# A state-space layer with a routed feed-forward block: chunk 0's second delta, gate projections and a later chunk's statistics go into the prologue, its taps into the steady order, and the gate's silu to step 8

## The reference, cut to what matters

```python
x = x + ssm(layernorm(x))      # x: 8 sequences x 1024 tokens x 256 features, fp32
x = x + ffn(layernorm(x))

def ssm(x):
    xp, z = split(x @ in_proj.T)                   # 512 channels each
    xc = silu(causal_conv(xp, conv_w))             # 4 taps per channel, along time
    dt, B, C = split(xc @ x_proj.T)                # 64, 16, 16 columns
    delta = softplus(dt @ dt_proj.T + dt_b)
    hs[t] = exp(delta * A) * hs[t-1] + delta * B * xc     # 512 channels x 16 states
    y = sum over the states (hs * C) + D * xc
    return (y * silu(z)) @ out_proj.T
```

## Time and profile before

| | before |
|---|---|
| median of 3 runs | 1596.67 us (1594.35 to 1600.29) |
| the profiled execution: time, span of its instructions | 1596.78 us, 1594.7 us |
| busy: DVE, PE, POOL, ACT | 93%, 91%, 88%, 79% |
| first scan starts (end of the prologue) | 40.73 us |
| first scan of chunk 1 starts | 148.48 us |

### The profile page before, as it was taken

One profiled execution on the slowest core, in us unless ns is written; L12 is line 12 of the kernel. 1 busy time (PEld: TensorE's weight loads), 2 busy tenths in 40 slices (PEclk: granted clock), 3 DMA queues, 4 the chain that ended last, 5 costly groups with the idle time before them and its releaser, 6 DMA issues.

```text
span 1594.7 us, 39330 instructions
## 1 busy us (share of the span) xinstructions
PE 1454.2 (91%) x15138; PEld 1124.9 (71%) x15138; DVE 1476.0 (93%) x1773; ACT 1257.9 (79%) x2100; POOL 1409.8 (88%) x1248
## 2 busy tenths in 40 slices
PE   7788999999999999999999999999999999998876
PEld 4466767677776777767777777777777777776765
DVE  4789999999999999999999999999999999998884
ACT  6778697897978879797887979789796987877651
POOL 2679899999989999899999989899998999999993
PEclk9999999999999999999999999999999999999998
DMA  4203013040320404022040311304031030403201
GB/s 136 80 2 112 23 29 134 3 160 2 95 68 3 159 3 147 15 69 94 3 159 3 130 32 43 120 3 160 2 101 61 16 133 3 147 1 93 69 15 41
DMA packets 78511, 106.46 MB, mean 67 GB/s; under 512 B 42289, under 2 KB 67761, under 8 KB 70130
## 3 DMA queue, kind: packets, MB, share of 16 engines
q1 hardware_dynamic: 78322, 103.92, 20.3%
HBM read 86.10 MB, written 17.30 MB: 65 GB/s over the span
## 4 chain that ended last, share of the span: by engine, by line
ACT 27%; DVE 25%; PE 23%; issue 15%; POOL 9%; SPq 1%; DVEq 0%; DMA 0%; ACTq 0%; POOLq 0%
DVE hs L919 22%; ACT da L586 12%; PE BX L233 9%; POOL hs L1203 6%; PE Y L257 3%; PE Y L282 3%; PE PB L357 2%; PE PB L330 2%; ACT xc L653 1%; ACT gate L647 1%; ACT u L691 1%; ACT L663 1%; ACT L662 1%; ACT u L689 1%; ACT u L693 1%
## 5 line engine op out<-in xcount | busy, mean ns | idle before, releaser
L1203 POOL TENSOR_TENSOR hs<-hs,cb 128x1024 f32<-128x1024 f32 x512 | 1209.8, 2364 | 70.3 <-DVE hs L919 49.6
L919 DVE TENSOR_TENSOR_SCAN hs<-da,BX 128x512 f32<-128x512 f32 x1024 | 1165.6, 1201 | 70.1 <-PE BX L233 61.4
L586 ACT ACTIVATE da<-delta,a_neg 128x511 f32<-128x511 f32 (+1 forms) x1024 | 665.3, 712 | 34.4 <-DVE hs L919 34.0
L257 PEld LDWEIGHTS Y<-ident,hs 128*128 128x128 f32 x4096 | 470.7, 142 | 95.7 <-issue 61.7
L257 PE MATMUL Y<-ident,hs 128*128 128x128 f32 x4096 | 518.5, 275 | 9.5 <-POOL hs L1203 9.3
L233 PE MATMUL BX<-bd,uT 32*128 32x128 f32 x8192 | 302.3, 284 | 91.0 <-DVE hs L919 86.9
L233 PEld LDWEIGHTS BX<-bd,uT 32*128 32x128 f32 x8192 | 253.2, 187 | 149.6 <-DVE hs L919 142.0
L282 PE MATMUL Y<-xnT,w_in 128*128 128x512 f32 x240 | 119.2, 620 | 2.1 <-ACT gate L639 2.0
L307 PE MATMUL PA<-w_in,xnT 128*128 128x512 f32 x240 | 115.6, 604 | 0.0
L621 ACT ACTIVATE xp<-Y 128x512 f32<-128x512 f32 x60 | 35.9, 598 | 93.5 <-PE Y L282 93.0
L1199 POOL COPY hlast<-hs 128x2 f32<-128x2 f32 x256 | 47.9, 187 | 55.8 <-DVE hs L919 54.0
(11 more groups left out here) (177 smaller groups left out, 1511.4 us busy)
## 6 DMA issues: line engine op xcount, KB each, us to landing
cb<-c_scratch SPq DMA_DIRECT2D x64, 1024.0 KB, 4.8
x<-in_x SPq DMA_DIRECT2D x16, 512.0 KB, 3.9
x_scratch<-x2T SPq DMA_DIRECT2D x16, 512.0 KB, 6.6
xt<-in_x SPq DMA_DIRECT2D x15, 512.0 KB, 4.0
bd<-bt SPq DMA_DIRECT2D x480, 1.0 KB
out<-x SPq DMA_DIRECT2D x15, 512.0 KB, 3.3
...
c_scratch<-dbc SPq DMA_DIRECT2D x64, 8.0 KB, 1.5
```

The lines of the kernel that those rows point to most:

```text
L257: mm = e.matmul(Y[(G * c + g) % 2][:, t * P:(t + 1) * P], hs[:, k % HR, q, t * P:(t + 1) * P], ident[:, :], is_transpose=True, start=False ...
L586: e.activation(da[:, k % DR, q, h:], delta[:, g, h:], ACT.Exp, scale=a_neg[:, g, n:n + 1]).then_inc(s_da, 1)
L919: e.tensor_tensor_scan(hs[:, k % HR, q, :], da[:, k % DR, q, :], BX[:, :].rearrange("p (t n) -> p n t", n=RT)[:, n % RT, :], float(c % HV) ...
L1203: e.tensor_tensor(hs[:, k % HR, :, :], hs[:, k % HR, :, :], cb[:, Q * p:Q * p + Q, :], ALU.mult).then_inc(s_hc, 1)
```

## The change

In the prologue, DVE's two memsets come first and no longer wait for the weights; ACT waits only for `w_conv` before the convolution, and its exponential of `A_log` stands behind the copy of `dbc`; PE runs 24 instead of 16 matmuls on the identity, transposes chunk 0 block by block as the norm hands it over, and runs three more on the identity. Delta of group 1 (into a bank of BX), its `pool_u`, the last two gate projections, the transposes of chunk 1 (now behind the first BX) and the statistics of chunk 3 are in the prologue or placed anew there. In chunk 0 the four projections stand at steps 0, 4, 8, 12 instead of 0, 2, 6, 12, and the taps are split: two at 1, 5, 9, 13 and the third at 3, 7, 9, 15. In every chunk the gate's silu moves from step 1 to step 8, the transposes of chunk c+2 from steps 3 and 5 to 2 and 3, `act_norm` from step 27 to 31, `pool_rstd` from 23 to 25.

```diff
-BANK_B = {0: [("o", -2, 0)], 2: [("ut", 0, 1)], 3: [("trc", 2, 0)], 4: [("yt", -1, 2)], 5: [("trc", 2, 1)], 6: [("dt", 0, 2)],
-          8: [("res", -1, 0)], 15: [("yt", 0, 0)], 16: [("dt", 0, 3)], 20: [("ut", 0, 3)], 21: [("yt", 0, 1)], 24: [("dt", 1, 0)],
+BANK_B = {0: [("o", -2, 0)], 2: [("ut", 0, 1), ("trc", 2, 0)], 3: [("trc", 2, 1)], 4: [("yt", -1, 2)], 6: [("dt", 0, 2)],
+          8: [("res", -1, 0)], 13: [("trc0", 2, 1)], 15: [("yt", 0, 0)], 16: [("dt", 0, 3)], 20: [("ut", 0, 3)], 21: [("yt", 0, 1)], 24: [("dt", 1, 0)],
...
+            if (stage, c, i) == ("dt", 0, 1):
+                return BX[:, CH:2 * CH], 0, s_d1, s_d1_out
...
+        def pe_trc_first(e):
+            for t in range(TB):
+                if t < TB - 1:
+                    e.wait_ge(s_xn0, t + 1)
+                else:
+                    e.wait_ge(s_xn, 1)
+                for kk in range(KD):
+                    mm = e.transpose((PB, PA)[kk][:, t * P:(t + 1) * P], xt[:, t, kk * P:(kk + 1) * P], ident[:, :])
+                    if t == TB - 1:
+                        mm.then_inc((s_pb, s_pa)[kk], 1)
...
-            for _ in range(16):
+            for _ in range(24):
...
-            pe_trc(e, 0, 0)
-            pe_trc(e, 0, 1)
+            pe_trc_first(e)
+            for _ in range(3):
+                e.matmul(Y[1][:, 0:P], ident[:, :], ident[:, :], start=True, stop=True)
...
-                    if c == 0 and s in (0, 2, 6, 12):
-                        pe_xp(e, (4, 5, 6, 7)[(0, 2, 6, 12).index(s)])
+                    if c == 0 and s in (0, 4, 8, 12):
+                        pe_xp(e, G + s // 4)
...
-                    if s == 3 and c and on(c + 2):
+                    if s == 2 and c and on(c + 2):
                         pe_trc(e, c + 2, 0)
...
-                    if s == 5 and c and on(c + 2):
+                    if s == 3 and c and on(c + 2):
                         pe_trc(e, c + 2, 1)
...
             act_norm(e, 1)
-            e.wait_ge(s_wt, 16 * 10)
...
+            e.wait_ge(s_wc, 16)
+            act_halo(e, 0)
+            act_xp_first(e, 0)
+            act_xp_first(e, 1)
+            e.preload_act_table(ACT.Silu)
+            act_silu_first(e, 0)
+            act_xp_first(e, 2)
+            act_xp_first(e, 3)
...
+            e.preload_act_table_set(EXPS)
+            act_dbc(e, 0)
...
                     if s == 1 and c:
                         act_z(e, c, 3)
-                        act_silu_z(e, c)
...
-                    if s == 1 and c == 0:
-                        act_silu_z(e, 0)
+                    if s == 8:
+                        act_silu_z(e, c)
...
-                    if s == 27 and on(c + 3):
+                    if s == 31 and on(c + 3):
                         act_norm(e, c + 3)
...
-                    if c == 0 and s == 1:
-                        dve_delta(e, 0, 1)
-                    if c == 0 and s in (1, 5, 9, 15):
-                        for kk in range(K - 1):
-                            dve_tap(e, (4, 5, 6, 7)[(1, 5, 9, 15).index(s)], kk)
+                    if c == 0:
+                        if s in (1, 5, 9, 13):
+                            dve_tap(e, G + s // 4, 0)
+                            dve_tap(e, G + s // 4, 1)
+                        if s in (3, 7, 9, 15):
+                            dve_tap(e, {3: G, 7: G + 1, 9: G + 2, 15: G + 3}[s], 2)
```

More of the change, by code:

```diff
@@ L69, in mamba_moe @@
     x2_dram = nc.dram_tensor("x2_scratch", (NQ, P, KD, CH), F32, kind="Internal").ap()
-    a_use = bank_uses(BANK_A, NQ, S, [("trc", 0, 1), ("trc", 1, 1), ("dbc", 0, 0), ("bt", 0, 0), ("dt", 0, 1)])
-    b_use = bank_uses(BANK_B, NQ, S, [("trc", 0, 0), ("trc", 1, 0), ("dt", 0, 0), ("ut", 0, 0)])
+    a_use = bank_uses(BANK_A, NQ, S, [("trc", 0, 1), ("dbc", 0, 0), ("bt", 0, 0), ("trc", 1, 1)])
+    b_use = bank_uses(BANK_B, NQ, S, [("trc", 0, 0), ("dt", 0, 0), ("ut", 0, 0), ("trc", 1, 0)])
     def on(c):
@@ L293, in pe_xp_first, with pe_z_first @@
             mm.then_inc(s_x0, 1)
-        def pe_z_first(e, t):
+        def pe_z_first(e, t, parts=range(2)):
             if t >= 2:
                 e.wait_ge(s_z0_out, t - 1)
-            for kk in range(KD):
+            for kk in parts:
                 mm = e.matmul(Y[t % 2][:, :], xnT[0][:, kk, t * P:(t + 1) * P], w_in[:, kk, ED:2 * ED], start=(kk == 0),
                               stop=(kk == KD - 1))
-            mm.then_inc(s_z0, 1)
+            if kk == KD - 1:
+                mm.then_inc(s_z0, 1)
         def pe_z(e, c, t):
@@ L328, in pe_dt @@
             e.wait_ge(out, n)
+            if (c, g) == (0, 1):
+                e.wait_ge(s_xc0, 2)
             e.wait_ge(s_pa_out, a_use["dbc", c, 0] + 1)
@@ L432, in tensor @@
             pe_dbc(e, 0, 1)
+            pe_z_first(e, 3, (0,))
             pe_dt(e, 0, 0)
             pe_bt(e, 0)
+            pe_dt(e, 0, 1)
+            pe_z_first(e, 3, (1,))
             pe_z_first(e, 2)
             pe_ut(e, 0, 0)
+            e.wait_ge(s_d1_out, 1)
             pe_bx(e, 0)
-            pe_dt(e, 0, 1)
-            pe_z_first(e, 3)
+            pe_trc(e, 1, 0)
+            pe_trc(e, 1, 1)
             for c in range(NQ):
@@ L755, in scalar @@
             e.wait_ge(s_ident, 1)
-            act_norm(e, 0)
+            e.wait_ge(s_sh, 1)
+            for t in range(TB):
+                e.activation(xt[:, t, :], xt[:, t, :], ACT.Identity, bias=shift[:, t:t + 1],
+                             scale=rstd[:, t:t + 1]).then_inc(s_xn0 if t < TB - 1 else s_xn, 1)
             act_trc(e, 0, 0)
@@ L795, in scalar @@
                         act_halo(e, 1)
-                    if c == 0 and s in (0, 2, 6, 12):
-                        act_xp(e, (4, 5, 6, 7)[(0, 2, 6, 12).index(s)])
+                    if c == 0 and s in (0, 4, 8, 12):
+                        act_xp(e, G + s // 4)
+                    if c == 0 and s == 0:
+                        act_exp(e, 3)
+                        act_exp(e, 4)
                     if s == 1 and c:
                         act_z(e, c, 3)
-                        act_silu_z(e, c)
                     if s == 2:
                         act_ut(e, c, 1)
+                    if s in (3, 4) and c and on(c + 2):
+                        act_trc(e, c + 2, s - 3)
                     if s == 4 and c and on(c + 1):
@@ L807, in scalar @@
                         act_yt(e, c - 1, 3)
-                    if s == 3 and c and on(c + 2):
-                        act_trc(e, c + 2, 0)
-                    if s == 5 and c and on(c + 2):
-                        act_trc(e, c + 2, 1)
                     if s == 6:
@@ L852, in scalar @@
                         act_exp(e, k + DR - 1)
-                    if s == 0:
+                    if s == 0 and c:
                         act_skip(e, c, 0)
-                    if s == 1 and c == 0:
-                        act_silu_z(e, 0)
+                    if s == 8:
+                        act_silu_z(e, c)
                     if s in (12, 13) and c == 0:
@@ L862, in scalar @@
                         act_skip(e, c, 1)
-                    if s == 10 and c == 0:
+                    if s == 5 and c == 0:
                         act_norm(e, 2)
@@ L1063, in vector @@
                             ALU.add).then_inc(s_mask, 1)
+            e.memset(w_dt[R:FX, :], 0.0).then_inc(s_wdt, 1)
+            e.memset(dbc[FX:FX + 1, :], 1.0).then_inc(s_wdt, 1)
             dve_stats(e, 0, 0)
@@ L1069, in vector @@
             dve_aggr(e, 1)
-            e.wait_ge(s_wt, 16 * 10)
-            e.memset(w_dt[R:FX, :], 0.0).then_inc(s_wdt, 1)
-            e.memset(dbc[FX:FX + 1, :], 1.0).then_inc(s_wdt, 1)
             e.wait_ge(s_mask, 1)
@@ L1079, in vector @@
             dve_aggr(e, 2)
+            dve_stats(e, 3, 0)
+            dve_stats(e, 3, 1)
             dve_bd(e, 0)
             dve_delta(e, 0, 0)
-            for p in range(1, NR):
-                dve_bd(e, p)
+            dve_bd(e, 1)
+            dve_delta(e, 0, 1)
+            dve_bd(e, 2)
+            dve_bd(e, 3)
             for c in range(NQ):
@@ L1142, in vector @@
                     if on(c + 3):
-                        if s == 9:
+                        if s == 9 and c:
                             dve_stats(e, c + 3, 0)
@@ L1275, in gpsimd @@
                         pool_times_c(e, k)
-                        if c == 0 and s == 1:
-                            pool_u(e, 0, 1)
                         if s == 7:
@@ L1290, in gpsimd @@
                         pool_gap(e, c - 1)
-                    if s == 23 and on(c + 3):
+                    if s == 25 and on(c + 3):
                         pool_rstd(e, c + 3)
```

54 lines of the change are left out of this document (22 added, 32 removed).

## The result

| | before | after |
|---|---|---|
| median of 4 runs each | 1597.93 us (1594.35 to 1600.29) | 1574.3 us (1572.66 to 1575.84) |
| the profiled execution: time, span | 1596.78, 1594.7 us | 1574.1, 1572.0 us |

The ratio of after to before is 0.9854, 95% interval 0.9831 to 0.9876: 1.5% faster, clear of the noise. The forecast was 1574.7.

What follows compares the result with a forecast made beforehand. DVE's scans with BX's refill set a floor of 5.85 us per pair of steps. Gains of 5.1 (prologue), 12.1 (chunk 0) and 4.9 (steady chunks) sum to 22.1 us off 1596.78: 1574.7, range 1570 to 1584.

Steps and rivals of the forecast that it cites:

- Prologue: Everything before the first scan: the chain starts earlier, first scan at 35.65 instead of 40.73, 5.1 us gained.
- rival (2): The clock does not hold: 1.75 + 0.8 us in the prologue, some 1.9 in the first pair; 1579.1, chance 0.19.
- Each beside the chain: Before the first scan: delta 1, two gate projections and chunk 3's statistics (1.4 on DVE) run beside the critical chain.
- Chunk 0: From the first scan to chunk 1: 2.05 us over the floor where it was 14.15, 12.1 us gained.
- no idle time to lose: POOL in the steady chunks: its statistics move past one product pair and one u without loss.
- Steady chunks: Pairs from steps 2 and 4: odd chunks gain 0.46, even 0.34, chunk 1 0.2; 4.9 us in all.
- The 0.07 left over: Pair of steps 2 and 3: two transposes and two sums end at 347.45, scans at 347.4; 0.07 us over allowed.
- Rival (3): Steady chunks gain nothing: both transposes ahead of one BX take 0.44 where uT gave 0.35 back; 1579.6, chance 0.17.
- Silu at step 8: ACT gets 4.5 us more against 3.59 idle; uT of step 10 loses nothing, 0.1 to spare plus some 0.3.
- Rival (4): uT of step 10 is late and PE waits; beyond 0.4 us, every us costs 15 in chunks 1 to 15; chance 0.03.
- The signs named: New profile: first scan 35.7, `dbc` 27.6, second pair 42.5, chunk 0 95.7 long, chunk 3 pairs at most 5.95.
- the late pair of even chunks: Pair set by POOL at the end of even chunks: might go, 0.5 us in each, towards the low end 1570.

Runs made afterwards that it cites:

- the other trace: Traced run of the kernel before with only the steady-chunk edits added, prologue code unchanged; median 1590.08 us, ratio 0.9962.
- start alone: Changed kernel with silu at step 1, transposes at 3 and 5, norm at 27, statistics at 23 again from chunk 1 on; 1580.16 us, 0.9905.
- norm at 27: Changed kernel with the norm back at step 27 and its POOL statistics at 23; 1574.49 us, 0.9853.
- the steady part alone: Kernel before plus silu at step 8, transposes at 2 and 3, norm at 31, statistics at 25 in every chunk; 1590.08 us, 0.9962.
- the run without the power: Changed kernel with POOL's power of -1/2 in the first layer norm replaced by a product from chunk 3 on; 1571.16 us, 0.9844.

## Why the prediction was right

The sum gave 22.1 us and the spans differ by 22.7. That it came this close is partly luck: chunk 0 gained 1.0 less than summed, the steady chunks 0.9 more and the end 0.8 more, and these cancel. Against the second execution of the changed kernel (span 1576.1) the same spans differ by 18.6. What held is the mechanism, term by term:

- **Prologue, 5.1 predicted, 4.98 measured.** First scan at 35.75 for 35.65, first tap 15.94 for 15.95, second load and `dbc` at 26.97 for 26.98. The clock held through the projections, and the experiment with fewer matmuls shows that the edit did it. Of rival (2)'s 2.55 in the prologue, the 1.75 for the projections came out at 1.16 there; its 0.8 for the first BX was not tried, since BX took 1.17 in that run too. "Each beside the chain" was not quite right: delta 1 stands ahead of DVE's last two `bd`, and BX waited for these (done at 34.49) and not for uT (there at 34.27). With the other trace's first scan at 40.07 the gain would be 4.3.
- **Chunk 0, 12.1 predicted, 11.13 measured.** First pair 0.81 over (0.95 predicted), steps 8 and 9 0.84 (0.86), pairs with two taps 0.05 each. Two things were missing: the second pair's 0.91, half clock after PE's wait of 2.51 us, which in other executions hits another instruction or none that matters; and 0.34 at steps 28 and 29, for POOL. The second is absent in both traces of the new start with the statistics at 23 and no pair of chunk 0 late by the clock (start alone, norm at 27), and it appears when the steady part alone is put into the kernel before (0 to 0.32), so it comes with their move to 25: "no idle time to lose" was right of the steady chunks and wrong of chunk 0. The sum had priced the falling clock as a rival in the first pair and nothing behind it.
- **Steady chunks, 4.9 predicted, 5.8 measured.** Odd chunks gained 0.53 for 0.46, even ones 0.41 for 0.34. The 0.07 left over for two transposes and two sums in one hole was not needed. The prediction took four scans as 4.5 us where the rows have 4.55, so by the earlier trace rows BX at 353.97 stands 0.29 behind the scans and not 0.35, and the hole at steps 2 and 3 reaches to 347.48; the sum does not hang on either. The two edits that were held responsible are: silu with norm 2.7, transposes 3.1, and the norm's move nothing. Rival (3) is excluded.
- **Silu at step 8: nothing predicted, nothing measured, with 0.40 us to spare** where 0.1 plus 0.3 was read from the rows. The total is right and its parts are not: 0.21 ahead of the output projection, so 0.19 behind it. Rival (4) did not happen, but its slope is real: 0.87 us more on ACT cost 0.47 in each chunk, and 2.66 us more made the kernel slower than before. By the Trainium skill's 2.66 us for a switch of table sets (ScalarE: Activation LUTs, What ACT_TABLE_LOAD costs) that rival would have come true. In the changed kernel loads and silu stand at 345.63, 346.93 and 348.86 with the next decay at 350.15, 4.52 us in all as in the earlier trace rows: the measurement decides.
- **The signs named.** First scan, `dbc` (done at 27.56), the second pair's start (42.42 for 42.5) and no pair of chunk 3 above 5.95 all came, and DVE in chunk 0 never waited for a decay. Two did not: chunk 0 is 96.62 long for 95.7, with its largest excess in the second pair and not at steps 1 and 9 (in the second execution, where that pair is punctual, it is at steps 8 and 9), and the copy of uT at step 10 ends 0.21 ahead of the projection and not under 0.1.
- **Chunk 14 to the end: nothing predicted, 0.8 measured.** This is no effect of the change. The second execution of the same kernel had 222.1 there and the first 218.0.

The range from 1570 upwards was rightly set for the low end: the late pair of even chunks, named there as the thing that could go, is 3.2 us in chunks 1 to 13, but this change does not touch it.

Not tried: the power taken off POOL in a way that keeps the norm right. By the run without the power I estimate it at about 3 us, if it adds no work elsewhere.
